# Causal mask of the self-attention scores: added by VectorE in the pass that takes each head's maximum, instead of by a mask product on TensorE, with the written-out orders laid out anew

## The chip, the core and the metric

The kernel runs on one core of one Trainium2 chip. The metric is the device time of one execution in microseconds (us); lower is better. The core has the engines TensorE (PE, with its weight loads PEld), VectorE (DVE), ScalarE (ACT), GpSimd (POOL) and SyncE (SP), which issues the transfers. They run side by side and meet at semaphores. In a steady stage the granted TensorE clock was 1.00, the 2.4 GHz level.

## What is computed

One decoder layer with layer norms behind the residual sums, for 16 batches of S = 112 rows, model width D = 256, 16 heads of 16, and a context of 375 rows per batch. Cut to what matters:

```python
# self-attention (scores already hold both of its terms and the scale)
causal = jnp.tril(jnp.ones((s, s), dtype=bool))
scores = jnp.where(causal[None, None], scores, -jnp.inf)
attn = jax.nn.softmax(scores, axis=-1)
out = jnp.einsum('bhqk,bkhd->bqhd', attn, V).reshape(b, s, H * hd)
# the layer
x = _layernorm(x + self_attention(x))
x = _layernorm(x + cross_attention(x, ctx, mask))       # keys 375, one mask for all rows
x = _layernorm(x + fp4_ffn(x))                          # blocks of 16 quantized before each product
```

## The kernel before

The work is a software pipeline over batches. In slot i the five engines work on several batches at once: self-attention of batch i+1 (`a`), the maxima of the cross-attention scores of batch i (`c`), the rest of the cross-attention of batch i-1 (`p`, `ct`), the first half of the feed-forward part of batch i-2 (`f`) and its end for batch i-3 (`ft`), while the projections of batch i+2 (`fr`) and the context keys and values of batch i+1 (`kv`) are made. Slots 3 to 13 run the same list (`slot`), the ramp (slots -2 to 2) and the drain (14 to 18) have lists of their own. Each engine has its own list, written out by hand in an order that was laid out beforehand, and works it off strictly in order; the numbers of slots and uses are known when the program is built, so every wait is on a constant.

Results of TensorE land in PSUM banks, shared in rings of two: `score` (raw scores), `prob` (scores with keys as rows), `misc` (everything else; its order of use is the table MISC_IN, MISC_ORDER, MISC_OUT). A use n of a ring may start when the reader of use n-2 has let go (`taken`), so the order of a ring ties TensorE to its readers.

Self-attention scores: heads come in four groups of four, A0 to A3. `bias_self(i, big)` writes the causal mask into the two banks of a pair of groups, as a product of an identity `identb` (bf16) and the mask `causal4` (bf16, 448 columns wide, four heads side by side), two matmuls of 448 columns. `scores_self` adds the eight head products of the pair onto it. VectorE then takes the maximum of each head's row, one reduction for a group of four heads (`max_self`). `turn_max` turns the maxima (misc use A.mT), ScalarE copies them to `mT`, GpSimd spreads them into `move_a` (`diagonal`), and a second score product with keys as rows (`turned_self`) subtracts them and masks by `shift_a`, before ScalarE takes the exponentials. The cross-attention does likewise with `max_cross`, which already adds its mask on VectorE: one custom instruction with an accumulated maximum (`tensor_tensor_reduce`) for each head of 375 columns, and a second, short one that reads the accumulator.

The feed-forward part's quantization is a chain of nine VectorE steps: `quant_x` for x (256 columns), whose end releases `turn_xq` (misc use X.xT), and `quant_h` for the two halves of h (352 columns), whose end releases `turn_hq` (hT1, hT0) of the next slot. `ctx_k` writes the context keys (K0, K1), which ScalarE copies to `kcf` and rounds, and VectorE subtracts (`ctxk_lo`).

The lines that the profile names most here: 1922 the mask product, 1933 the self scores, 1254 the self maxima, 1262 the cross maxima and their accumulator reads, 1980 the turned maxima, 2041 the context keys, 2062 the turns of xq, hq, x and att, 1162 to 1180 the quantization steps, 1344 the layer norm before it, 1310 the residual sums, 1291 the low half of xq, 633 the spreading on GpSimd.

## Time and profile before

| | |
|---|---|
| median of 3 runs | 662.46 us (661.29 to 663.1) |
| time of the profiled execution | 661.05 us |
| its span, first to last instruction | 659.2 us |
| PE busy | 592.7 us (90%) in 5682 matmuls |
| VectorE busy | 509.9 us (77%) in 1555 instructions |
| ScalarE, GpSimd busy | 294.6 us, 213.8 us |
| steady slots 3 to 13 | about 35.6 us each |

A busy PE is a modelled figure: the matmuls are pipelined, and their ends overlap with the next one's start, so the time that a piece of work costs the PE is read from start to start. What matters is what the PE waits for, slot by slot.

### The profile page before, as it was taken

Reading aid. Unit: us, or ns where it says so; the run is one execution under the profiler, and the core shown is the slowest. Engines: PE = TensorE matmul, PEld = TensorE weight load, DVE = VectorE, ACT = ScalarE, POOL = GpSimd, SP = SyncE. Lnnn points to the kernel's source line nnn. Section 1 sums busy time; section 2 is a strip of 40 time slices with the busy share of each in tenths; the row PEclk is TensorE's granted clock in tenths of the full one; section 3 lists DMA queues with packets and bytes.
Section 4 is the critical chain, followed back from the end, with each engine's and each line's share of the span. In section 5 each row is a group of like instructions: output and inputs, shape, how many; then the busy total and the mean of one; then the engine's idle time right before and its main releaser. Section 6 shows DMA issues by size and latency. Waiting matters only on the chain.

```text
span 659.2 us, 16222 instructions
## 1 busy us (share of the span) xinstructions
PE 592.7 (90%) x5682; PEld 380.1 (58%) x5682; DVE 509.9 (77%) x1555; ACT 294.6 (45%) x717; POOL 213.8 (32%) x286
## 2 busy tenths in 40 slices
PE   3687798899999999999999999999999999997964
PEld 3445465566666666666666656665666665553532
DVE  3679688896978869696968687887969696979772
ACT  1144354445454555454545455454545454442411
POOL 5244234315150524242341515051424233223001
PEclk9789899899999999999999999999999999999996
DMA  6734461515252433526251525343342512120000
GB/s 168 212 95 138 140 191 49 175 32 150 75 152 86 132 107 74 164 56 178 54 143 59 158 70 151 87 133 106 91 148 59 173 50 88 49 88 2 9 7 14
DMA packets 64464, 67.78 MB, mean 103 GB/s; under 512 B 11696, under 2 KB 55936, under 8 KB 64384
## 3 DMA queue, kind: packets, MB, share of 16 engines
q1 hardware_dynamic: 64384, 66.75, 35.1%
q8 instruction: 46, 0.75, 0.5%
q14 instruction: 34, 0.28, 0.1%
HBM read 39.72 MB, written 27.00 MB: 101 GB/s over the span
## 4 chain that ended last, share of the span: by engine, by line
PE 64%; DVE 20%; issue 8%; ACT 3%; POOL 3%; SPq 1%; DMA 1%; DVEq 0%; POOLq 0%; ACTq 0%
PE misc L2020 18%; PE prob L1960 7%; PE misc L2101 6%; PE misc L2041 5%; PE xpv L2001 5%; PE misc L2012 5%; PE score L1946 5%; DVE junk L1262 4%; PE prob L1955 4%; DVE amax L1254 2%; PE apv L1989 2%; PE misc L2054 2%; PE misc L2062 2%; DVE qt L1176 2%; DVE hq L1180 1%
## 5 line engine op out<-in xcount | busy, mean ns | idle before, releaser
L1262 DVE CUSTOM_DVE_ANT_0 junk<-score,maskbias 112x375 bf16<-112x375 f32 x256 | 128.5, 540 | 43.3 <-PE score L1946 42.8
L800 ACT ACTIVATE xP<-prob 128x448 f32<-128x448 f32 (+1 forms) x192 | 98.5, 542 | 106.8 <-PE prob L1960 106.5
L638 POOL TENSOR_TENSOR rstd<-veps,half 112x1 f32<-112x1 f32 x48 | 27.2, 576 | 295.9 <-DVE veps L1340 295.9
L2020 PE MATMUL misc<-wguT,xqT 128*112 128x352 f32 x256 | 87.2, 468 | 0.5 <-ACT xqT L764 0.5
L633 POOL TENSOR_TENSOR move_a<-mT,negeye 16x448 bf16<-16x448 f32 x64 | 60.6, 969 | 77.9 <-ACT mT L764 77.9
L633 POOL TENSOR_TENSOR move_x<-mT,negeye 16x448 bf16<-16x448 f32 x64 | 65.3, 1036 | 53.9 <-ACT mT L764 53.9
L2020 PEld LDWEIGHTS misc<-wguT,xqT 128*112 128x112 f32 x256 | 44.2, 180 | 24.6 <-issue 2.9
L1960 PE MATMUL prob<-move_x,shift_x 128*128 128x448 bf16 x192 | 54.0, 360 | 1.5 <-POOL move_x L633 1.4
L2020 PE MATMUL misc<-xwvT_s,ctxT_s 128*128 128x256 f32 (+1 forms) x192 | 52.2, 395 | 0.0
L2101 PE MATMUL misc<-wdT,hqT 128*112 128x256 f32 x192 | 49.6, 402 | 1.5 <-ACT hqT L764 1.5
L1946 PE MATMUL score<-xK,xQ 64*128 64x375 f16 x256 | 42.9, 329 | 6.7 <-DVE xmax L1262 6.2
L2001 PE MATMUL xpv<-xP,xV 128*32 128x112 f32 (+1 forms) x1536 | 47.9, 264 | 0.0
L2041 PE MATMUL misc<-ctxT_s,xwkT_s 128*128 128x375 f32 x128 | 47.7, 494 | 0.1
L2001 PEld LDWEIGHTS xpv<-xP,xV 128*32 128x32 f32 (+1 forms) x1536 | 36.5, 110 | 8.9 <-issue 8.1
L1254 DVE TENSOR_REDUCE amax<-score 112x4 f32<-112x448 f32 x64 | 37.6, 612 | 4.0 <-PE score L1933 4.0
L2101 PEld LDWEIGHTS misc<-wdT,hqT 128*112 128x112 f32 x192 | 32.8, 184 | 13.5 <-issue 6.8
L1946 PEld LDWEIGHTS score<-xK,xQ 64*128 64x128 f16 x256 | 13.1, 92 | 46.5 <-issue 32.0
L793 ACT ACTIVATE aP<-prob 112x448 f32<-112x448 f32 x64 | 31.6, 541 | 17.4 <-PE prob L1960 13.3
L1955 PE MATMUL prob<-xQ,xK 64*128 64x112 f16 x768 | 35.4, 212 | 1.9 <-ACT xP L800 1.9
L2020 PEld LDWEIGHTS misc<-xwvT_s,ctxT_s 128*128 128x128 f32 (+1 forms) x192 | 32.6, 187 | 7.7 <-issue 2.4
L1178 DVE TENSOR_TENSOR qt<-qt 112x352 f32<-112x352 f32 (+4 forms) x56 | 33.7, 602 | 0.9
L764 ACT ACTIVATE kcf<-misc 128x375 f32<-128x375 f32 x32 | 15.5, 483 | 36.2 <-PE misc L2041 36.2
(163 smaller groups left out, 1117.5 us busy)
## 6 DMA issues: line engine op xcount, KB each, us to landing
xk_dram<-xk_parts SPq DMA_DIRECT2D x64, 192.0 KB, 3.1
xK<-xk_dram SPq DMA_DIRECT2D x16, 768.0 KB, 4.6
ctxT_s<-in_ctxT SPq DMA_DIRECT2D x16, 375.0 KB, 3.8
aq_dram<-aq_parts SPq DMA_DIRECT2D x64, 64.0 KB, 2.6
ak_dram<-ak_parts SPq DMA_DIRECT2D x64, 64.0 KB, 2.1
aQ<-aq_dram SPq DMA_DIRECT2D x16, 256.0 KB, 3.6
aK<-ak_dram SPq DMA_DIRECT2D x16, 256.0 KB, 2.8
xq_dram<-xq_parts SPq DMA_DIRECT2D x64, 64.0 KB, 2.1
```

What stands on the lines that cost most here:

```text
L633: pool.tensor_tensor(dst[0:H, heads, :], mT[:, n].unsqueeze(1).to_broadcast([H, GH, S]), negeye[:, heads].unsqueeze(2).to_broadcast([H, GH ...
L800: act.activation(xP[0:KEYS[c], g % 2, c], prob[m][0:KEYS[c], 0:GH * S].rearrange("p (h q) -> p h q", h=GH), ACT.Exp).then_inc(probs.taken[ ...
L1178: done(dve.tensor_tensor(t1, t1, t2, ALU.subtract))
L1254: dve.tensor_reduce(amax[:, b.par, GH * g:GH * g + GH], score[m][0:S, 0:GH * S].rearrange("p (h k) -> p h k", h=GH), AX.X, ALU.max).then_i ...
L1262: dve.tensor_tensor_reduce(junk[:, m], score[m][0:S, 0:SC], maskbias[:], 1.0, -3.0e38, ALU.add, ALU.max, xmax[:, b.par, h:h + 1]).then_inc ...
L1946: pe.matmul(score[m[a]][:, 0:SC], xQ[rows_, b.par, at, :], xK[rows_, b.par, at, 0:SC], start=True, stop=True).then_inc(scores.full[m[a]], 1)
L1955: pe.matmul(prob[m[a]][:, n * S:(n + 1) * S], K[rows_, b.par, DT * n + big, keys], Q[rows_, b.par, DT * n + big, 0:S], start=(n == 0), sto ...
L1960: pe.matmul(prob[m[a]][:, 0:GH * S], shift_[:, keys], move[:, GH * g:GH * g + GH].rearrange("p h q -> p (h q)"), start=False, stop=True).t ...
L2001: mm = pe.matmul(xpv[VW * h:VW * h + VW, g * S:(g + 1) * S], xV[0:k, b.par, c, GH * g + h, :], xP[0:k, g % 2, c, h, :], start=(g == 0 and ...
L2020: mm = pe.matmul(misc[m][0:rows_, 0:cols], actT(c), weightT(c), start=(c == 0), stop=(c == DT - 1))
L2041: mm = pe.matmul(misc[m][:, 0:SC], xwkT_s[:, c, t * P:(t + 1) * P], ctxT_s[:, b.par, c, :], start=(c == 0), stop=(c == DT - 1))
L2101: mm = pe.matmul(misc[m][0:S, 0:D], hqT[0:k, c, :], wdT[0:k, c, :], start=(c == 0), stop=(c == IC - 1))
```

## The change

`bias_self`, `identb` and `causal4` are gone. `scores_self` now starts each bank itself, and waits itself for the banks to be free. `max_self` issues four custom instructions per group, one for each head of 112 columns, which add the 112x112 mask `causal` and take the maximum, each with its accumulator read; `junk` is widened to hold what they write. The orders of all engines, in ramp, slot and drain, and the table of the misc ring are new. SP's list moves too: in the slot, the load of x comes first, the fetch of aQ ahead of that of aK, and the store of y now stands ahead of the fetches of xK and xQ. Cut to the core:

```diff
-                pool.affine_select(out=causal4[:], in_=causal4[:], compare_op=ALU.is_ge, fill=NEG, base=0,
-                                   pattern=[[0, GH], [-1, S]], channel_multiplier=1).then_inc(consts, 1)
+                pool.affine_select(out=causal[:], in_=causal[:], compare_op=ALU.is_ge, fill=NEG, base=0,
+                                   pattern=[[-1, S]], channel_multiplier=1).then_inc(consts, 1)
...
...
 
             def max_self(i, b, g):
                 m = scores.wait_full(dve, i, f"A{g}")
-                dve.tensor_reduce(amax[:, b.par, GH * g:GH * g + GH],
-                                  score[m][0:S, 0:GH * S].rearrange("p (h k) -> p h k", h=GH),
-                                  AX.X, ALU.max).then_inc(scores.taken[m], 1)
+                for n in range(GH):
+                    h, cols = GH * g + n, slice(n * S, n * S + S)
+                    mx = dve.tensor_tensor_reduce(junk[:, m, cols], score[m][0:S, cols], causal[:], 1.0, -3.0e38, ALU.add,
+                                                  ALU.max, amax[:, b.par, h:h + 1])
+                mx.then_inc(scores.taken[m], 1)
...
-            def bias_self(i, big):
-                for a in range(2):
-                    m = scores.wait_free(pe, i, f"A{BIG * big + a}")
-                    pe.matmul(score[m][:, 0:GH * S], identb[:], causal4[:].rearrange("p h k -> p (h k)"),
-                              start=True, stop=False)
-
             def scores_self(i, b, big):
                 if big == 0:
                     pe.wait_ge(aq_in[b.par], b.round(16, 16))
                     pe.wait_ge(ak_in[b.par], b.round(16, 16))
-                m = [scores.at(i, f"A{BIG * big + a}")[0] for a in range(2)]
+                m = [scores.wait_free(pe, i, f"A{BIG * big + a}") for a in range(2)]
                 for n in range(GH):
                     for a in range(2):
                         rows_ = slice(HALF * a, HALF * a + HALF)
                         mm = pe.matmul(score[m[a]][:, n * S:(n + 1) * S], aQ[rows_, b.par, DT * n + big, :],
-                                       aK[rows_, b.par, DT * n + big, 0:S], start=False, stop=(n == GH - 1))
+                                       aK[rows_, b.par, DT * n + big, 0:S], start=True, stop=True)
                         if n == GH - 1:
...
-MISC_ORDER = ["hT1", "hT0", "q", "down", "A.mT", "X.xT", "k", "gate0", "up0", "v", "gate1", "up1", "A.out",
-              "A.att", "K0", "A.o", "V0", "X.out", "K1", "X.att", "V2", "X.o", "A.xT", "X.mT", "V1", "A.q"]
+MISC_ORDER = ["hT1", "q", "hT0", "down", "A.mT", "X.xT", "k", "gate0", "v", "up0", "gate1", "up1", "A.out", "K0",
+              "A.att", "A.o", "V0", "X.out", "K1", "X.att", "V2", "X.o", "A.xT", "X.mT", "A.q", "V1"]
...
```

In the slot's list of VectorE (`slot`), its head and its tail:

```diff
                 max_self(i, a, 0)
+                layernorm(f)
                 max_self(i, a, 1)
-                layernorm(f)
                 quant_x(f, 0)
                 quant_x(f, 1)
+                q_lo(i, fr)
                 quant_x(f, 2)
+                max_self(i, a, 2)
                 quant_x(f, 3)
-                max_self(i, a, 2)
+                max_self(i, a, 3)
                 quant_x(f, 4)
-                max_self(i, a, 3)
-                q_lo(i, fr)
...
-                quant_h(i, f, 1, 4)
+                ctxk_lo(i, kv, 0)
+                quant_h(i, f, 0, 7)
                 ctxk_lo(i, kv, 1)
                 max_cross(i, c, 7)
                 residual_cross(i, ct)
-                quant_h(i, f, 1, 5)
+                quant_h(i, f, 1, 7)
+                moments(i, ct, 1, "X.o", 0)
+                moments(i, ct, 1, "X.o", 1)
                 quant_h(i, f, 0, 8)
-                quant_h(i, f, 1, 6)
-                moments(i, ct, 1, "X.o", 0)
-                quant_h(i, f, 1, 7)
-                moments(i, ct, 1, "X.o", 1)
                 quant_h(i, f, 1, 8)
                 moments(i, ct, 1, "X.o", 2)
                 xq_lo_(i, a)
```

TensorE at the seam of two steady slots, before (from the turn of the cross maxima, `ident,xmax`, over the mask product to the second pair of self scores and what follows):

```order
L1980 MATMUL misc<-ident,xmax 16x112
L2020 MATMUL misc<-xwvT_s,ctxT_s 128x256 x2
L2012 MATMUL misc<-x1T,xwqT_s 128x112 x4
L1922 MATMUL score<-causal,identb 128x448 x2
L1933 MATMUL score<-aK,aQ 128x112 x8
L1955 MATMUL prob<-xQ,xK 128x112 x8
L1960 MATMUL prob<-move_x,shift_x 128x448 x2
L2062 MATMUL misc<-ident,hq 128x112
L2062 MATMUL misc<-ident,hq 64x112
L2062 MATMUL misc<-ident,hq 128x112 x4
L1922 MATMUL score<-causal,identb 128x448 x2
L1933 MATMUL score<-aK,aQ 128x112 x8
```

The same place in the changed kernel:

```order
L1973 MATMUL misc<-ident,xmax 16x112
L2005 MATMUL misc<-x1T,xwqT_s 128x112 x4
L2013 MATMUL misc<-xwvT_s,ctxT_s 128x256 x2
L1926 MATMUL score<-aK,aQ 128x112 x8
L1948 MATMUL prob<-xQ,xK 128x112 x8
L1953 MATMUL prob<-move_x,shift_x 128x448 x2
L2055 MATMUL misc<-ident,hq 128x112
L2055 MATMUL misc<-ident,hq 64x112
L2005 MATMUL misc<-xT_s,wqT_s 128x112 x4
L2055 MATMUL misc<-ident,hq 128x112 x4
L1994 MATMUL xpv<-xP,xV 32x112 x8
L1926 MATMUL score<-aK,aQ 128x112 x8
```

Both mask products are gone, the q projection (`xT_s,wqT_s`) and one cross value product (`xP,xV`) now stand between the first and the second pair of self scores, and the projection from x1T stands ahead of the values from ctxT.

VectorE at the same seam, before (from the cross residual `res` to the first two groups of self maxima `amax`):

```order
L1310 TENSOR_TENSOR res<-misc,x1kept 112x256
L1174 TENSOR_SCALAR qt<-qt 112x352
L1180 TENSOR_TENSOR hq<-qt,qscale 112x352
L1176 SCALAR_TENSOR_TENSOR qt<-qt 112x352
L1332 BN_STATS stats<-res 112x6
L1178 TENSOR_TENSOR qt<-qt 112x352
L1336 BN_AGGR mv<-stats 112x2
L1180 TENSOR_TENSOR hq<-qt,qscale 112x352
L1340 TENSOR_SCALAR veps<-mv 112x1
L1291 SCALAR_TENSOR_TENSOR xq_parts<-misc,xq_parts 128x2x112
L1254 TENSOR_REDUCE amax<-score 112x4 x2
```

The same place in the changed kernel (the last two rows come four times for each group):

```order
L1309 TENSOR_TENSOR res<-misc,x1kept 112x256
L1175 TENSOR_TENSOR qt<-qt 112x352
L1331 BN_STATS stats<-res 112x6
L1335 BN_AGGR mv<-stats 112x2
L1177 TENSOR_TENSOR hq<-qt,qscale 112x352 x2
L1339 TENSOR_SCALAR veps<-mv 112x1
L1290 SCALAR_TENSOR_TENSOR xq_parts<-misc,xq_parts 128x2x112
L1253 ISA junk,amax<-score,causal 112x112
L1253 ISA amax 112x1
```

The rows 1174 and 1176 of the second half of h (1171 and 1173 by the changed file's numbers) are gone from this tail; both `hq` steps now stand together, behind `mv`.

VectorE ahead of it, around the context keys, before:

```order
L1336 BN_AGGR mv<-stats 112x2
L1340 TENSOR_SCALAR veps<-mv 112x1 x2
L1301 RECIPROCAL rsum<-misc 112x16
L1262 ISA junk,xmax<-score,maskbias 112x375
L1262 ISA xmax 112x1
L1262 ISA junk,xmax<-score,maskbias 112x375
L1262 ISA xmax 112x1
L1304 TENSOR_TENSOR att<-misc,rsum 112x256
L1171 TENSOR_SCALAR qt<-qt 112x352
L1285 TENSOR_TENSOR xk_parts<-kcf,xk_parts 128x375
```

In the changed kernel:

```order
L1335 BN_AGGR mv<-stats 112x2
L1339 TENSOR_SCALAR veps<-mv 112x1
L1171 TENSOR_SCALAR qt<-qt 112x352
L1300 RECIPROCAL rsum<-misc 112x16
L1339 TENSOR_SCALAR veps<-mv 112x1
L1173 SCALAR_TENSOR_TENSOR qt<-qt 112x352 x2
L1303 TENSOR_TENSOR att<-misc,rsum 112x256
L1284 TENSOR_TENSOR xk_parts<-kcf,xk_parts 128x375
L1175 TENSOR_TENSOR qt<-qt 112x352
L1284 TENSOR_TENSOR xk_parts<-kcf,xk_parts 128x375
```

The two steps gone from the tail are here now, with two steps of the first half of h, between the two parts of the cross normalisation (`rsum`, `att`), and the seventh pair of cross maxima (`max_cross(i, c, 6)`) that stood between them has moved ahead.

## Rows read from the trace of the kernel before

**Rows 1.** The page's busy times: engine, us, share of the span, instructions.
```profile
PE 592.7 (90%) x5682; PEld 380.1 (58%) x5682; DVE 509.9 (77%) x1555; ACT 294.6 (45%) x717; POOL 213.8 (32%) x286
```

**Rows 2.** Windows: us, busy of PE, PEld, DVE, ACT, POOL; clock, DMA share, GB/s.
```profile
333.30:368.80 35.50, 34.81 (x353) 22.70 (x352) 28.36 (x92) 17.86 (x44) 11.90 (x16) 1.00 0.38 109
```

**Rows 3.** The chain that ended last: the down product, slots 3 and 12.
```profile
190.96 2.77 PE misc L2101 x12
...
511.39 2.77 PE misc L2101 x12
```

**Rows 4.** Groups by form: busy us, mean ns of one, idle before.
```profile
L1262 DVE CUSTOM_DVE_ANT_0 junk<-score,maskbias 112x375 bf16<-112x375 f32 x256 | 128.5, 540 | 43.3 <-PE score L1946 42.8 <-issue 0.2
...
L1254 DVE TENSOR_REDUCE amax<-score 112x4 f32<-112x448 f32 x64 | 37.6, 612 | 4.0 <-PE score L1933 4.0
...
L1262 DVE DVE_READ_ACCUMULATOR2_ANT xmax<- 112x1 f32 x256 | 21.1, 82 | 0.0
...
L1922 PE MATMUL score<-causal,identb 112*128 112x448 bf16 x64 | 20.2, 363 | 4.1 <-DVE amax L1254 4.1
```

**Rows 5.** PE in order of time: start us, us, what; [idle before, releaser].
```profile
336.87 0.36 PE L2062 MATMUL misc<-ident,xq 112*128 112x112 f32 x2
...
342.74 1.34 PE L2001 MATMUL xpv<-xP,xV 128*32 128x112 f32 x48
...
357.12 1.53 PE L2041 MATMUL misc<-ctxT_s,xwkT_s 128*128 128x375 f32 x4
...
361.89 0.26 PE L1980 MATMUL misc<-ident,xmax 112*16 112x112 f32 x1 [0.48 <-DVE res L1310]
...
363.74 0.54 PE L1922 MATMUL score<-causal,identb 112*128 112x448 bf16 x2
364.22 0.37 PE L1933 MATMUL score<-aK,aQ 64*128 64x112 f16 x8
...
366.06 0.36 PE L1922 MATMUL score<-causal,identb 112*128 112x448 bf16 x1
366.60 0.36 PE L1922 MATMUL score<-causal,identb 112*128 112x448 bf16 x1 [0.17 <-DVE amax L1254]
366.89 0.37 PE L1933 MATMUL score<-aK,aQ 64*128 64x112 f16 x8
```

**Rows 6.** VectorE in order of time, the same columns.
```profile
334.07 0.57 DVE L1269 SCALAR_TENSOR_TENSOR aq_parts<-misc,bq_s,aq_parts 128x112 f16<-128x112 f32 x2
...
342.55 0.55 DVE L1262 CUSTOM_DVE_ANT_0 junk<-score,maskbias 112x375 bf16<-112x375 f32 x1 [2.11 <-PE score L1946]
...
343.02 0.54 DVE L1262 CUSTOM_DVE_ANT_0 junk<-score,maskbias 112x375 bf16<-112x375 f32 x1
```

**Rows 7.** VectorE at the seam of two slots.
```profile
361.32 0.42 DVE L1310 TENSOR_TENSOR res<-misc,x1kept 112x256 f32<-112x256 f32 x1
361.66 0.24 DVE L1174 TENSOR_SCALAR qt<-qt 112x352 bf16<-112x352 bf16 x1
361.82 0.52 DVE L1180 TENSOR_TENSOR hq<-qt,qscale 112x352 f32<-112x352 f32 x1
362.25 0.52 DVE L1176 SCALAR_TENSOR_TENSOR qt<-qt 112x352 f32<-112x352 f32 x1
...
363.03 0.92 DVE L1178 TENSOR_TENSOR qt<-qt 112x352 f32<-112x352 f32 x1
...
363.98 1.14 DVE L1180 TENSOR_TENSOR hq<-qt,qscale 112x352 f32<-112x352 f32 x1
...
365.40 1.14 DVE L1254 TENSOR_REDUCE amax<-score 112x4 f32<-112x448 f32 x2
366.46 0.40 DVE L1344 TENSOR_SCALAR x<-res,mv,rstd 112x256 f32<-112x256 f32 x1
...
371.27 0.42 DVE L1180 TENSOR_TENSOR xq<-qt,qscale 112x256 f32<-112x256 f32 x1
```

**Rows 8.** GpSimd at the seam.
```profile
362.52 2.21 POOL L633 TENSOR_TENSOR move_x<-mT,negeye 16x448 bf16<-16x448 f32 x2 [2.01 <-ACT mT L764]
```

More of the change, by code:

```diff
@@ L663, in ramp @@
                 residual(at[0])
-                residual(at[1])
                 power(0, at[0])
@@ L1617, in slot @@
                 k_lo(i, fr)
+                moments(i, ft, 2, "down", 0)
+                moments(i, ft, 2, "down", 1)
                 gate_(i, f, 0)
@@ L1788, in drain @@
                 quant_x(at[14], 6)
+                moments(at[15], at[12], 2, "down", 1)
                 quant_x(at[14], 7)
@@ L1794, in drain @@
                 quant_h(at[16], at[14], 0, 1)
+                moments(at[15], at[12], 2, "down", 2)
                 quant_h(at[16], at[14], 0, 2)
@@ L1820, in drain @@
                 moments(at[16], at[15], 1, "X.o", 2)
+                moments(at[16], at[13], 2, "down", 1)
                 layernorm(at[15])
@@ L2386, in drain @@
                 pv_cross(at[15], at[14], 0, 0)
-                turned_cross(at[15], at[14], 0, 2)
+                pv_cross(at[15], at[14], 0, 1)
                 turn_hq(at[15], at[12], "hT1", range(4, IC))
                 turn_hq(at[15], at[12], "hT0", range(4))
-                pv_cross(at[15], at[14], 0, 1)
+                turned_cross(at[15], at[14], 0, 2)
+                down(at[15], at[12])
+                turn_xq(at[15], at[13])
+                gate_up(at[15], at[13], "gate", 0)
+                gate_up(at[15], at[13], "up", 0)
```

874 lines of the change are left out of this document (426 added, 448 removed), and 14 rows, old and new, of tables (MISC_IN, MISC_OUT).

## The prediction, on record before the changed kernel ran

> **What bounds the kernel now.** I read the page's busy times first, then a steady slot by windows, then the chain that ended last, then TensorE and VectorE in order of time around one seam of two slots. The page gives TensorE 90% of the span and VectorE 77% [rows 1]. That is an average, so the second view is one slot: in 35.50 us TensorE is busy for 34.81 at a granted clock of 1.00, its 2.4 GHz level, and VectorE for 28.36 [rows 2]. The chain has the same down product at 190.96 in slot 3 and at 511.39 in slot 12, nine periods of 35.60 us on average [rows 3]. Eleven such slots, 3 to 13, are 392 of the 659 us.
>
> Inside a slot TensorE waits twice in a way that the trace names: 0.48 us before the turned cross maxima, for the bank that the cross residual lets go, and 0.17 us before the second mask product of the second pair, for a self maximum [rows 5]. So the slot is TensorE's, but with little in hand over VectorE. How little, the reader sees in one loop through both engines, which I call the loop:
> - TensorE turns xq at 336.87 and comes to the end of the second context key product, K1, at 357.12 + 1.53 = 358.65: 21.78 us [rows 5].
> - From K1 ScalarE's copies and VectorE's tail lead to the next xq. It is done at 371.27 + 0.42 = 371.69: 13.04 us after K1 [rows 5, 7]. Some 0.05 us of semaphore bring it to TensorE.
> - Together 34.87 us. The period is 35.6, so the loop has 0.7 us of slack now, and TensorE does not wait for xq.
>
> **What goes from TensorE.** The first pair's mask product takes from 363.74 to the start of the self scores at 364.22, 0.48 us; the second pair's from 366.06 to 366.89, 0.83 us, its wait included [rows 5]. I leave about 0.1 us of each to the switch into the self scores, which stays: 1.1 us a slot. A TensorE that nothing else held up would have a period of 34.5 us. The scores products themselves keep number and size.
>
> **What comes to VectorE.** A reduction over a group is 612 ns long, but two stand from 365.40 to 366.46, so one costs 0.53 us [rows 4, 7]. The new form, 112 columns, has no row. The same instruction at 375 columns is 540 ns long and costs 0.47 us from start to start, its accumulator read of 82 ns included [rows 4, 6]. What a column costs I take from this instruction and a 256-column sum from PSUM, 0.34 us from 361.32 to 361.66 [rows 7]: 0.13 us for 119 columns, 1.1 ns each. 263 columns fewer leave 0.47 - 0.27 to 0.29, about 0.20 us. The bounds: if cost were proportional to columns, 0.47 x 112 / 375 = 0.14; the nearest row of this width, two operations of 112 columns that also read a bias, is 0.57 us for both with the tail of the last, 0.285 each at most, some 0.24 from start to start if that tail is as long as in the other rows [rows 6]. I take 0.20, since the opcode is the one with the 0.47. A group then costs 0.80, +0.27; four groups, +1.08 us a slot. The added instructions wait for nothing: the group's one wait stays ahead of its first.
>
> The Trainium skill, Perfetto Trace Analysis, section Optimizing Scalar/DVE Operations, speaks against this change: it gives a DVE instruction on PSUM about 125 ns of overhead and advises grouping into larger operations. By it a group of four would cost 0.97 us, and the slot would come out as in the slower rival below; this trace sides with less, 0.47 us where 375 columns by the page would be 0.52.
>
> **What the new order does to the loop.** All four groups, the layer norm and q's low half lie between the tail and xq in both orders, so the whole +1.08 is in the loop; only their order differs. The tail loses the two steps L1174 and L1176, 0.16 and 0.43 us [rows 7]. But GpSimd's first two spreads run from 362.52 to 364.73 [rows 8], and in that time the step L1178 is 0.92 us and the last hq 1.14, where the hq before them is 0.52 [rows 7]. In the new order both hq stand there and L1178 ahead of it: 0.6 more, 0.4 less. Net the tail is 0.35 shorter. The steps put ahead of K1's residue lie in time that VectorE has: it needs 28.4 + 1.1 = 29.5 of 35 us. On TensorE one value product moves out of the stretch from xq to K1, across the seam; three take 1.34 us, so about 0.40 goes [rows 5]. The loop is then 13.04 + 0.05 - 0.35 + 1.08 = 13.82 and 21.78 - 0.40 = 21.38, together 35.20 us. That is above TensorE's 34.5: TensorE will wait for xq about half a microsecond a slot, and the gain is 35.60 - 35.20 = 0.40, not 1.1. Eleven slots: -4.4 us.
>
> The first value product and the q projection between the two pairs of self scores, about 1.3 us of TensorE work, are there to cover the maxima of the first pair, 1.6 + 0.4 us with the layer norm between them. Where they fall short, TensorE waits for a second maximum, but the same delay is then missing at xq. The wait of 0.48 for the residual stays, since nothing between K1 and it has changed.
>
> **SP.** In the slot the store of y stands ahead of the fetches of xK and xQ now. It waits for the last layer norm, behind it both fetches wait. That layer norm is on ScalarE before the low half of xq is, for which the put ahead of the store waits anyhow; I add one issue and nothing to the time, since the cross scores that read both fetches come behind the k and v projections, a gate and an up product of the next slot. If that cover were gone, it would cost the issue, under half a microsecond a slot. The fetch of aQ and aK feeds the next slot, the load of x the one after.
>
> **Ramp and drain.** The page's idle TensorE time is 659.2 - 592.7 = 66.5 us [rows 1]; eleven slots of 0.7 hold 8 of it, so the rest lies in ramp and drain. There five batches have a mask product. Were TensorE the bound, they would give back 5 x 1.1 = 5.5 us; were VectorE, which also quantizes the weights there, they would cost 5 x 1.08 = 5.4. The reordering has no price in any row. I take -1, and these two as bounds.
>
> **Sum.** -4.4 - 1 = -5.4 on the profiled execution's 661.05 us (span 659.2 and 1.85 around it): 655.6. The median of the runs lies 1.4 above that execution, so 657 us.
>
> **Rivals.**
> 1. *The loop closes early, TensorE stays the bound.* For it: 0.14 us per instruction instead of 0.20 takes 16 x 0.06 = 0.96 off the loop, 34.2, below 34.5. Against it: fixed parts are seen in every short VectorE row. 11 x -1.1 = -12.1, with -1 outside: 649.5.
> 2. *Slower, by the price of the small instruction.* The loop breaks even at 0.40 / 16 = 0.025 us more than I take, 0.225 us each. At 0.24, as the operations with a bias suggest, it is 35.20 + 0.64 = 35.84, +0.24 a slot, +2.6 in eleven; with VectorE-bound ramp and drain of +1 to +5 the result is 666 to 670. Its place is the group of self maxima and then the wait for xq.
> 3. *No change.* Either the price is 0.21 to 0.225, or ramp and drain give back what the slots gain: 661 to 664.
> 4. *The freed TensorE time was covered.* If the mask product ran while TensorE had to wait anyhow, nothing is freed; the rows show it issued right behind the projection and the turned h, so only its 0.17 is such time. I count this with no change.
>
> **How the numbers follow.** A change under 0.3%, 2 us, can't be told from none here. Forecast 654 to 660.4: 0.44. Rival 1, 649 to 654: 0.17. No change, 660.5 to 664.5: 0.19. Slower: 0.20. So faster 0.61, same 0.19, slower 0.20. The range of 650 to 666 takes in the TensorE bound below and the 0.24 price above; the forecast's own is 654 to 660.
>
> **What would show it.** The custom instruction of 112 columns at about 0.20 us from start to start, 270 ns long; down products 35.2 us apart in the chain; TensorE waits before the turn of xq, released by xq; that of 0.48 unchanged; VectorE near 29.5 busy in a slot. Wrong would be: no wait at xq and a period of 34.5 (rival 1), or a long one and a period over 35.6 (rival 2), or a period as forecast with the difference in ramp or drain.

## Result: slower by 1.3%, and the profile after

The changed kernel takes 672.12 us (median of 4 runs, 670.18 to 675.07), the kernel before 662.78 us on the same chip (661.29 to 665.74). The ratio is 1.0131, 95% interval 1.0107 to 1.0155. The forecast was 657 us, within 650 to 666, with a chance of 0.20 for slower. It was wrong in direction and in range.

The profiled execution took 672.86 us, its span is 671.1 us. First the page of the changed kernel, its busy times and the group of the masked maxima:

```profile
span 671.1 us, 16558 instructions
PE 592.5 (88%) x5618; PEld 375.2 (56%) x5618; DVE 531.0 (79%) x2003; ACT 296.7 (44%) x717; POOL 219.7 (33%) x284
L1253 DVE CUSTOM_DVE_ANT_0 junk<-score,causal 112x112 bf16<-112x112 f32 x256 | 53.5, 264 | 2.4 <-PE score L1926 2.3
```

VectorE has 21 us more to do, as [rows 1] and this line show side by side. TensorE's busy time hardly moved (592.7 to 592.5), though the mask products are gone. In a steady slot at a granted clock of 1.00 it went from 34.80 us (301.38 to 336.87, before) to 34.51 (308.83 to 344.65), and over the whole execution the mean granted clock was 0.952 here and 0.970 there. Busy is a modelled figure, so it does not price what was taken out; how the rest divides between model and clock is not shown.

From the chain that ended last, the same projection from x1 (the one that starts with `misc<-x1T,xwqT_s`) in two slots nine periods apart, start and length:

```profile
190.27 0.91 PE misc L2005 x8
...
513.04 0.91 PE misc L2005 x8
```

(513.04 - 190.27) / 9 = 35.86 us, against 35.60 in [rows 3]. The first of the nine is still 36.19 long, the others are 35.82. A slip in the numbering ahead of the result: the down products at 190.96 and 511.39 in the kernel before belong to slots 4 and 13; nine periods lie between them all the same, and slots 3 to 13 are eleven.

VectorE of the changed kernel at the seam of two slots, in order of time (start, length, line and operation, waits in brackets), which answers to [rows 7]:

```profile
333.10 0.42 DVE L1309 TENSOR_TENSOR res<-misc,x1kept 112x256 f32<-112x256 f32 x1
333.44 0.52 DVE L1175 TENSOR_TENSOR qt<-qt 112x352 f32<-112x352 f32 x1
...
334.49 2.28 DVE L1177 TENSOR_TENSOR hq<-qt,qscale 112x352 f32<-112x352 f32 x2
336.70 0.14 DVE L1339 TENSOR_SCALAR veps<-mv 112x1 f32<-112x1 f32 x1
336.76 0.38 DVE L1290 SCALAR_TENSOR_TENSOR xq_parts<-misc,xq_parts 128x224 f16<-128x224 f32 x1
337.06 0.26 DVE L1253 CUSTOM_DVE_ANT_0 junk<-score,causal 112x112 bf16<-112x112 f32 x1
337.25 0.08 DVE L1253 DVE_READ_ACCUMULATOR2_ANT amax<- 112x1 f32 x1
337.25 0.26 DVE L1253 CUSTOM_DVE_ANT_0 junk<-score,causal 112x112 bf16<-112x112 f32 x1
...
343.75 0.42 DVE L1177 TENSOR_TENSOR xq<-qt,qscale 112x256 f32<-112x256 f32 x1
344.09 0.42 DVE L1309 TENSOR_TENSOR res<-misc,x 112x256 f32<-112x256 f32 x1
```

And TensorE and GpSimd in the same seam:

```profile
328.90 1.53 PE L2034 MATMUL misc<-ctxT_s,xwkT_s 128*128 128x375 f32 x4
...
334.30 2.10 POOL L630 TENSOR_TENSOR move_x<-mT,negeye 16x448 bf16<-16x448 f32 x2 [0.57 <-ACT mT L761]
337.29 0.38 PE L2055 MATMUL misc<-ident,hq 112*128 112x112 f32 x2 [0.48 <-DVE xq_parts L1290]
...
343.97 1.87 POOL L630 TENSOR_TENSOR move_a<-mT,negeye 16x448 bf16<-16x448 f32 x2 [4.66 <-ACT mT L761]
344.65 0.38 PE L2055 MATMUL misc<-ident,xq 112*128 112x112 f32 x2 [0.26 <-DVE res L1309]
```

Three things are to be read here. The masked maximum starts every 0.195 us (337.06, 337.25), so its price was forecast well. xq is done at 344.17, 13.74 us after K1's end at 330.43; forecast were 13.77. But TensorE turns xq at 344.65 only. What it waits for last is not xq but `res`, the residual of the FFN's output (FFN: the feed-forward part), which stands behind the last step of xq on VectorE. This residual reads the `misc` bank that the turn of xq needs, since a use of the ring may start when the reader of the use two before has let go, and `down` is that use. So the loop closes through the residual, 0.48 us behind xq: 14.22 + 21.60 = 35.82 us, which is the period.

### The profile page after: what moved, and what is told of

Read it like the earlier page. It is cut to its first block, busy times and chain, and to the rows that moved or that the text cites. A ratio compares the mean times of both kernels' runs of the same rounds, so it can differ in the third digit from the quotient of the medians.

```text
span 671.1 us, 16558 instructions
## 1 busy us (share of the span) xinstructions
PE 592.5 (88%) x5618; PEld 375.2 (56%) x5618; DVE 531.0 (79%) x2003; ACT 296.7 (44%) x717; POOL 219.7 (33%) x284
## 4 chain that ended last, share of the span: by engine, by line
PE 56%; DVE 29%; issue 7%; ACT 4%; POOL 1%; SPq 1%; DMA 1%; DVEq 0%; POOLq 0%; ACTq 0%
PE misc L2013 18%; PE misc L2034 6%; DVE junk L1253 6%; PE prob L1953 6%; PE score L1939 5%; PE xpv L1994 5%; PE misc L2005 5%; DVE junk L1261 4%; PE prob L1948 3%; DVE hq L1177 3%; PE misc L2055 2%; PE apv L1982 2%; DVE res L1309 2%; PE misc L2047 2%; DVE qt L1175 2%
## 5 line engine op out<-in xcount | busy, mean ns | idle before, releaser
L1261 DVE CUSTOM_DVE_ANT_0 junk<-score,maskbias 112x375 bf16<-112x375 f32 x256 | 130.0, 546 | 44.6 <-PE score L1939 44.1
L797 ACT ACTIVATE xP<-prob 128x448 f32<-128x448 f32 (+1 forms) x192 | 95.6, 541 | 76.2 <-PE prob L1953 75.9
L635 POOL TENSOR_TENSOR rstd<-veps,half 112x1 f32<-112x1 f32 x48 | 29.8, 620 | 301.0 <-DVE veps L1339 301.0
L630 POOL TENSOR_TENSOR move_a<-mT,negeye 16x448 bf16<-16x448 f32 x64 | 62.5, 1000 | 73.8 <-ACT mT L761 73.8
L630 POOL TENSOR_TENSOR move_x<-mT,negeye 16x448 bf16<-16x448 f32 x64 | 63.4, 1005 | 58.3 <-ACT mT L761 58.3
L1953 PE MATMUL prob<-move_x,shift_x 128*128 128x448 bf16 x192 | 56.1, 366 | 0.4 <-POOL move_x L630 0.4
L2013 PE MATMUL misc<-xwvT_s,ctxT_s 128*128 128x256 f32 (+1 forms) x192 | 53.7, 403 | 2.5 <-DVE res L1309 2.2
L1253 DVE CUSTOM_DVE_ANT_0 junk<-score,causal 112x112 bf16<-112x112 f32 x256 | 53.5, 264 | 2.4 <-PE score L1926 2.3
L2034 PE MATMUL misc<-ctxT_s,xwkT_s 128*128 128x375 f32 x128 | 49.9, 514 | 0.4
L1277 DVE SCALAR_TENSOR_TENSOR ak_parts<-misc,bk_s,ak_parts 128x112 f16<-128x112 f32 x32 | 9.2, 328 | 30.7 <-ACT ak_parts L761 30.7
```

The source lines that it names most:

```text
L630: pool.tensor_tensor(dst[0:H, heads, :], mT[:, n].unsqueeze(1).to_broadcast([H, GH, S]), negeye[:, heads].unsqueeze(2).to_broadcast([H, GH ...
L797: act.activation(xP[0:KEYS[c], g % 2, c], prob[m][0:KEYS[c], 0:GH * S].rearrange("p (h q) -> p h q", h=GH), ACT.Exp).then_inc(probs.taken[ ...
L1253: mx = dve.tensor_tensor_reduce(junk[:, m, cols], score[m][0:S, cols], causal[:], 1.0, -3.0e38, ALU.add, ALU.max, amax[:, b.par, h:h + 1])
L1261: dve.tensor_tensor_reduce(junk[:, m, 0:SC], score[m][0:S, 0:SC], maskbias[:], 1.0, -3.0e38, ALU.add, ALU.max, xmax[:, b.par, h:h + 1]).th ...
L1953: pe.matmul(prob[m[a]][:, 0:GH * S], shift_[:, keys], move[:, GH * g:GH * g + GH].rearrange("p h q -> p (h q)"), start=False, stop=True).t ...
L2013: mm = pe.matmul(misc[m][0:rows_, 0:cols], actT(c), weightT(c), start=(c == 0), stop=(c == DT - 1))
```

## Experiments

Every kernel below keeps the reference's whole computation. "Mask" says which engine adds the causal mask, "order" whose written-out lists are used. I write "order of before" and "new order" for the written-out lists and the ring's table; K1 and "turn" (of xq, on TensorE) as in the prediction. The times are medians, and each ratio is to the kernel before on the same chip. The last four columns are medians over slots 4 to 12 of one profiled execution, worked out from the rows in order of time, as above; they are good to about 0.03 us.

| kernel | mask, order | time, us | ratio (95%) | K1 to xq done | xq done to turn | turn to K1 | period |
|---|---|---|---|---|---|---|---|
| before | TensorE, before | 662.8 to 664.2 | | 13.04 | 0.72 | 21.78 | 35.55 |
| changed | VectorE, new | 672.12 | 1.0131 (1.0107 to 1.0155) | 13.74 | 0.48 | 21.60 | 35.82 |
| old_order_dve_mask | VectorE, before | 685.3 | 1.0325 (1.0287 to 1.0363) | 15.00 | 0.48 | 21.76 | 37.24 |
| old_order_both | both, before | 676.17 | 1.0192 (1.0149 to 1.0235) | 14.27 | 0.48 | 21.76 | 36.52 |
| new_order_pe_mask | TensorE, new | 669.21 | 1.0075 (1.0049 to 1.0101) | 13.19 | 0.91 | 21.57 | 35.67 |
| old_ends_new_slot | VectorE, new slot only | 666.38 | 1.0044 (1.0025 to 1.0062) | 13.74 | 0.48 | 21.60 | 35.82 |
| old_dve_xq_first | VectorE, before, edited | 683.7 | 1.0304 (1.0261 to 1.0348) | 13.78 | 1.52 | 21.73 | 37.06 |
| new_resid | VectorE, new, edited | 668.97 | 1.0089 (1.0057 to 1.0121) | 13.94 | 0.06 | 21.62 | 35.62 |
| early_hq | VectorE, new, edited | 662.72 | 0.9986 (0.9967 to 1.0006) | 13.07 | 0.48 | 21.59 | 35.15 |
| before_early_hq | TensorE, before, edited | 660.84 | 0.9956 (0.9933 to 0.9979) | 12.99 | 0.48 | 21.81 | 35.31 |
| new_ramp | VectorE, new but for the drain | 668.56 | 1.0084 (1.0062 to 1.0106) | 13.73 | 0.49 | 21.60 | 35.82 |
| new_drain | VectorE, new but for the ramp | 668.37 | 1.0073 (1.0051 to 1.0095) | 13.74 | 0.48 | 21.60 | 35.83 |
| best2 | VectorE, old ends, slot edited | 657.43 | 0.9916 (0.9894 to 0.9937) | 13.28 | 0.06 | 21.63 | 34.97 |
| best2_pe | TensorE, as best2 | 660.30 | 0.9954 (0.9935 to 0.9973) | 13.69 | 0.06 | 21.62 | 35.37 |

### The exchange alone, the order alone

**old_order_dve_mask**: the changed kernel's functions, all lists and the ring's table of before, without the mask product's calls.

```diff
-MISC_ORDER = ["hT1", "q", "hT0", "down", "A.mT", "X.xT", "k", "gate0", "v", "up0", "gate1", "up1", "A.out", "K0",
-              "A.att", "A.o", "V0", "X.out", "K1", "X.att", "V2", "X.o", "A.xT", "X.mT", "A.q", "V1"]
+MISC_ORDER = ["hT1", "hT0", "q", "down", "A.mT", "X.xT", "k", "gate0", "up0", "v", "gate1", "up1", "A.out",
+              "A.att", "K0", "A.o", "V0", "X.out", "K1", "X.att", "V2", "X.o", "A.xT", "X.mT", "V1", "A.q"]
...
```

> The mask moved to VectorE as in the change, but every engine keeps the order of before. Theory 1, the loop that closes over the misc bank: in before TensorE turns xq 13.40 + 0.14 us after K1 at the earliest, since its bank is let go by the feed-forward residual behind xq, and 21.78 us later K1 is done, 35.3 against a period of 35.6. The four groups add 16 x 0.20 - 4 x 0.53 = 1.08 us, so the period becomes 36.4 and eleven slots cost +9, with 0 to +4 in ramp and drain: 670 to 676 us. Rival, TensorE is the bound and the new order alone is to blame: the 1.1 us of mask product per slot come back, 650 to 660 us.

**old_order_both**: the kernel before, with its mask product, and the masked maxima as well (the mask is added twice, which leaves the result as it is).

```diff
-                dve.tensor_reduce(amax[:, b.par, GH * g:GH * g + GH],
-                                  score[m][0:S, 0:GH * S].rearrange("p (h k) -> p h k", h=GH),
-                                  AX.X, ALU.max).then_inc(scores.taken[m], 1)
+                for n in range(GH):
+                    h, cols = GH * g + n, slice(n * S, n * S + S)
+                    mx = dve.tensor_tensor_reduce(junk[:, m, cols], score[m][0:S, cols], causal4[:, 0], 1.0, -3.0e38, ALU.add,
+                                                  ALU.max, amax[:, b.par, h:h + 1])
+                mx.then_inc(scores.taken[m], 1)
```

> The order of before with its mask product on TensorE kept, and the maxima taken as in the change (the mask is added twice, the result is the same). Only the price of the small VectorE instructions is added. Theory 1: the mask product lies outside the stretch from xq to K1, so the period is the same 36.4 as without it, and the time is within 3 us of the kernel of old order with the mask on VectorE alone, 672 to 678 us. Rival, TensorE bound: it is 12 us or more slower than that kernel.

Both are slower than the changed kernel, and the one that still has TensorE's mask product is 9 us the faster of the two. My expectation missed the first by 9 us (670 to 676); it had the second's time (672 to 678), but not its distance from the first (within 3 us). No count of "less work on TensorE, more on VectorE" gives that. The rows do. In old_order_dve_mask, the last step of xq and GpSimd's first spread of the self maxima:

```profile
309.27 0.92 POOL L630 TENSOR_TENSOR move_a<-mT,negeye 16x448 bf16<-16x448 f32 x1 [4.84 <-ACT mT L761]
309.32 1.15 DVE L1177 TENSOR_TENSOR xq<-qt,qscale 112x256 f32<-112x256 f32 x1
310.40 0.41 DVE L1309 TENSOR_TENSOR res<-misc,x 112x256 f32<-112x256 f32 x1
```

The same in old_order_both:

```profile
307.89 0.42 DVE L1180 TENSOR_TENSOR xq<-qt,qscale 112x256 f32<-112x256 f32 x1
308.04 2.85 POOL L633 TENSOR_TENSOR move_a<-mT,negeye 16x448 bf16<-16x448 f32 x3 [5.04 <-ACT mT L764]
308.24 0.42 DVE L1312 TENSOR_TENSOR res<-misc,x 112x256 f32<-112x256 f32 x1
```

Issued 0.05 us behind the spread's start, the step takes 1.15 us; issued 0.15 us ahead of it, 0.42 us. That is 0.73 us in each such slot, all of the difference of the periods (37.24 - 36.52 = 0.72) and, over eleven slots, 8 of the 9 us. Without its mask product TensorE is earlier at the turned maxima, so the spread is, and it meets the step. The 0.97 us that the masked maxima alone cost (36.52 - 35.55) are nearly the 1.08 us that the forecast put into the loop: the loop had little slack before.

One slot of old_order_dve_mask gives the counter-test inside a single execution. There the step happened to be issued 0.04 us ahead of the spread:

```profile
346.61 0.43 DVE L1177 TENSOR_TENSOR xq<-qt,qscale 112x256 f32<-112x256 f32 x1
346.65 2.06 POOL L630 TENSOR_TENSOR move_a<-mT,negeye 16x448 bf16<-16x448 f32 x2 [4.93 <-ACT mT L761]
```

It took 0.43 us, and TensorE turned xq 36.55 us after the turn before, where the slots on either side have 37.24. The lists are the same in all of them, so neither the order nor the missing mask product explains the 0.7 us; only the step's place against the spread differs.

The Trainium skill, SBUF — State Buffer, section Who interferes with whom, has the rule: a VectorE instruction with two inputs in SBUF contends with a GpSimd instruction that reads SBUF, whichever issues first keeps the shared port for its whole length and the other is blocked, and one with at most one SBUF input does not contend unless it runs in a mode that uses both of VectorE's ports, which `tensor_scalar` can enter. The rows agree in kind: 0.87 us were left of a spread of 0.92 us when the step came, and it ended 0.73 us late, somewhat less than a full block would make it, while the masked maxima, whose scores lie in PSUM, keep their 0.195 us in the changed kernel's spreads from 337.45 on. The layer norm's product, a `tensor_scalar` from SBUF to SBUF, is slowed too (0.69 to 1.11 us in all kernels but before, instead of 0.40); in which mode it ran no trace shows.

**new_order_pe_mask**: the new order with the functions of before, the mask product right ahead of the score products.

```diff
+                bias_self(i, 0)
                 scores_self(i, a, 0)
```

> The orders of the change, but with the mask product on TensorE (right ahead of each pair of self scores) and one reduction per group, as before. Theory 1: the loop is 35.8 - 1.1 = 34.7 us, so TensorE sets a period of 35.3 to 35.7 again and the slots cost nothing; what ramp and drain lost in the change by their order stays, what they lost by VectorE's work goes: 662 to 670 us. Rival, the order of the slots is at fault: a period of 35.8 or more stays, 670 us or more.

669.21 us: in the new order the exchange is worth +0.15 us a slot (35.82 against 35.67), and at the same time the order alone is 5 us slower than that of before (669.21 against 664.18). **old_ends_new_slot**, the changed kernel with ramp and drain in the order of before, tells where:

> The changed kernel with the ramp and the drain of the old order (the mask product left out of them) and the slot of the new order. Theory 1: the slots keep a period of 35.82, +2.4 us in eleven; the rest of the change's +12, 6.3 in the ramp and 3.6 in the drain, is by the order of these lists and goes but for the VectorE work of five batches, at most 5 us: 664 to 670 us. Rival, the ends lose by VectorE's work and not by order: 670 to 674 us, as the changed kernel.

666.38 us: 5.7 us of the 9.3 lie in the order of ramp and drain.

### Ramp and drain

**new_ramp** and **new_drain** each give one end back. Their edits are the lists and MISC_OUT, or MISC_IN, of before.

> The changed kernel's slot and first stretch (its ramp), with the drain in the order of before. Together with old_ends_new_slot (both ends of before, 666.38 us) and the changed kernel (both ends new, 672.1 us) it splits the 5.7 us that the ends' order costs. From the profiled executions: drain behind slot 13's down product 151.6 us in the changed kernel, 148.8 us in old_ends_new_slot (2.8 us), down product of slot 3 at 160.90 and 158.47 us (2.4 us). Theory 1: the two ends lose about half each, so 668 to 670.5. Rival (the first stretch's difference lies in the clock that one execution was granted, and the drain holds all of it): within 1 us of 666.4.

> The opposite: first stretch of before, slot and drain of the changed kernel. Theory 1: 668 to 670.5 as well, the two losses adding up to 5.7 us. Rival (the drain holds all of it): 671 to 673.

Against old_ends_new_slot the new ramp costs 0.40% (1.0084 against 1.0044) and the new drain 0.29%, some 2.7 and 1.9 us, each give or take 1.9; both together, in the changed kernel, 0.87%, 5.8 us give or take 2. So they fit the first theory, about half in each end; the exact split these runs can't tell.

What the loss consists of the traces show in part. The windows view (length, busy time of PE, PEld, DVE, ACT, POOL, granted clock, DMA share, GB/s), changed kernel:

```profile
40.00:80.00 40.00, 31.16 (x226) 20.20 (x225) 30.62 (x104) 15.48 (x37) 8.97 (x13) 0.84 0.50 138
80.00:120.00 40.00, 36.04 (x401) 23.06 (x402) 35.03 (x150) 20.14 (x49) 16.95 (x20) 0.90 0.39 110
...
580.00:620.00 40.00, 32.46 (x258) 17.97 (x256) 32.38 (x94) 14.18 (x33) 9.92 (x14) 0.87 0.20 57
```

The kernel before:

```profile
40.00:80.00 40.00, 31.88 (x222) 20.10 (x222) 30.07 (x80) 15.42 (x37) 10.84 (x14) 0.96 0.49 143
80.00:120.00 40.00, 36.38 (x449) 23.58 (x447) 34.52 (x92) 22.37 (x54) 20.64 (x22) 1.00 0.41 115
...
580.00:620.00 40.00, 34.52 (x359) 19.61 (x356) 30.08 (x92) 16.31 (x40) 10.03 (x12) 0.96 0.13 38
```

And new_drain, whose drain has the same lists as the changed kernel's:

```profile
580.00:620.00 40.00, 30.56 (x294) 16.77 (x298) 34.08 (x95) 14.84 (x34) 11.64 (x12) 1.00 0.20 57
```

From slot 13's down product to the end the changed kernel takes 151.6 us (519.51 to 671.1) and new_drain, by the same lists, 149.1 (517.51 to 666.6); the difference goes with the clock, 0.87 against 1.00. The lists of before take 148.8 in old_ends_new_slot. The ramp is alike: slot 3's down product starts at 160.90 in the changed kernel and at 158.19 in new_ramp, by the same lists. In the kernel before it starts at 154.63 and in before_early_hq, whose ramp is the same list for list, at 158.49, and there too the clocks differ. These are before_early_hq's windows, to be laid beside the kernel before's 0.96 and 1.00:

```profile
40.00:80.00 40.00, 32.75 (x208) 19.90 (x206) 28.03 (x75) 14.62 (x35) 10.28 (x13) 0.84 0.49 144
80.00:120.00 40.00, 36.60 (x384) 24.04 (x383) 31.97 (x91) 19.54 (x48) 17.77 (x17) 0.92 0.36 104
```

So the execution that stands ahead of the prediction had a fortunate ramp, and the lower clock of the changed kernel's ramp is no proof against its order. All executions together say more about the ends: the mean granted clock is 0.945 to 0.959 in the changed kernel's four and 0.963 to 0.970 in the ten of old_ends_new_slot. In new_order_pe_mask, with the new ends, three runs at 0.969 to 0.975 took 665.3 to 666.2 us, the other seven, at 0.953 to 0.962, 668.6 to 671.5. New_drain is at 0.964 to 0.974 and still takes 666.5 to 669.5. How much of the 5.7 us is waiting, how much the lower clock, and which brings the other about, these runs don't separate.

### The slot

**old_dve_xq_first** tests the collision: old_order_dve_mask, with xq's last steps ahead of the next q's low half.

```diff
                 max_self(i, a, 3)
-                q_lo(i, fr)
                 quant_x(f, 5)
                 quant_x(f, 6)
                 quant_x(f, 7)
                 quant_x(f, 8)
+                q_lo(i, fr)
```

> This is old_order_dve_mask (the order of before, mask added by VectorE), with the two parts of the next q (0.57 us) moved in VectorE's slot from ahead of the last four steps of the FFN input's quantizing to behind them. In old_order_dve_mask the last of these steps took 1.15 us, where it takes 0.42 us in the kernels before and old_order_both; it is issued 0.05 us after GpSimd has begun a spread (309.32 and 309.27), while in old_order_both it starts 0.15 us ahead of the spread. Theory 1 (a two-input VectorE instruction on on-chip float32 that is issued during a spread runs at under half its speed, and one issued ahead of it does not): the step starts 0.5 us earlier, falls back to 0.42 us, the slot shortens by about 0.7 to 1.2 us, and 685.3 us becomes 672 to 678. Rival (the missing mask product on TensorE is itself what costs old_order_dve_mask its 9 us over old_order_both): the time stays at 683 to 687.

The time stayed at 683.7 us, as the rival had it, yet not for its reason:

```profile
350.06 0.42 DVE L1177 TENSOR_TENSOR xq<-qt,qscale 112x256 f32<-112x256 f32 x1
350.41 0.57 DVE L1268 SCALAR_TENSOR_TENSOR aq_parts<-misc,bq_s,aq_parts 128x112 f16<-128x112 f32 x2
351.12 0.26 PE L1973 MATMUL misc<-ident,amax 112*16 112x112 f32 x1 [1.19 <-DVE aq_parts L1268]
351.75 3.60 POOL L630 TENSOR_TENSOR move_a<-mT,negeye 16x448 bf16<-16x448 f32 x4 [6.09 <-ACT mT L761]
352.00 0.36 PE L2055 MATMUL misc<-ident,xq 112*128 112x112 f32 x2
```

The step is back at 0.42 us and xq is done 1.22 us sooner behind K1 (13.78 against 15.00): 0.73 for the step, and about 0.5 since the parts of q now stand behind it. TensorE has no use for it: ahead of the turn of xq it turns the maxima, whose bank the low half of q has to release, and that is late now by 1.19 us. The step's own part of the theory holds, its effect on the time does not: the gain went into a new wait.

**new_resid**: the changed kernel, with the wait that the forecast missed taken away.

```diff
-                quant_x(f, 8)
                 residual_ffn(i, ft)
+                quant_x(f, 8)
```

> The changed kernel with one pair swapped in VectorE's slot: the residual of the FFN's output stands ahead of the last quantizing step of the next FFN input, not behind it. TensorE's turn of that input waited 0.26 us for this residual behind the step (344.09 with 0.42 us, turn at 344.65). Theory 1 (the collision with GpSimd's spread decides): the last step is then issued at about 344.1, after the spread's start at 343.97, and takes 1.15 instead of 0.42 us; the slot grows by about 0.6 us and the time goes to 676 to 681. Rival (the residual's wait is what the slot lost, and taking it away gives it back): the period falls from 35.8 to 35.6 or less, 668 to 671.

My theory lost. The step started 0.01 us ahead of the spread, not 0.13 behind it, and was not slowed:

```profile
340.91 0.42 DVE L1309 TENSOR_TENSOR res<-misc,x 112x256 f32<-112x256 f32 x1
341.24 0.41 DVE L1177 TENSOR_TENSOR xq<-qt,qscale 112x256 f32<-112x256 f32 x1
341.25 3.87 POOL L630 TENSOR_TENSOR move_a<-mT,negeye 16x448 bf16<-16x448 f32 x4 [4.66 <-ACT mT L761]
341.71 0.20 PEld L2055 LDWEIGHTS misc<-ident,xq 112*128 112x128 f32 x2 [0.48 <-DVE xq L1177]
```

TensorE waits for xq itself now and turns it 0.06 us after. The period fell by 0.20 us, to 35.62, so the wait for the residual behind xq was real and in the loop.

**early_hq**: the changed kernel, with both last steps of h ahead of the spreads.

```diff
                 quant_h(i, f, 0, 7)
+                quant_h(i, f, 0, 8)
                 ctxk_lo(i, kv, 1)
                 max_cross(i, c, 7)
                 residual_cross(i, ct)
                 quant_h(i, f, 1, 7)
+                quant_h(i, f, 1, 8)
                 moments(i, ct, 1, "X.o", 0)
                 moments(i, ct, 1, "X.o", 1)
-                quant_h(i, f, 0, 8)
-                quant_h(i, f, 1, 8)
```

> The changed kernel with the last quantizing step of both halves of h moved ahead in VectorE's slot: the first half's into the idle 0.27 us ahead of the second part of xk, the second half's straight behind the step ahead of it, so that both are issued ahead of GpSimd's spreads at 334.30. Now the two take 2.21 us from issue to the next one, unslowed 0.43 us each. Theory 1 (VectorE's tail of the slot lies on the loop, so what the spreads cost there counts): 1.1 to 1.4 us less on VectorE in each slot; the period falls from 35.8 until another limit ends it, at 34.6 to 35.3; time 660 to 667. Rival (the loop is TensorE's, and the tail only fills its waits): 670 to 673.

9.4 us less from moving two lines, period 35.15. The slots make 7.4 us of it (11 times 0.67); in this execution the drain was also shorter, 148.4 us from slot 13's down product (512.73) to the end against 151.6, by the same lists and at a granted clock of 1.00 against 0.87 from 580 to 620 us. Of the 1.35 us saved on the two steps (2.21 to twice 0.43), 0.67 reached the period; part of the rest was paid back at once, since the layer norm's product, also from SBUF to SBUF, now falls into the second pair of spreads and takes 1.02 us instead of 0.69:

```profile
331.36 0.53 DVE L1177 TENSOR_TENSOR hq<-qt,qscale 112x352 f32<-112x352 f32 x1
331.60 1.97 POOL L630 TENSOR_TENSOR move_x<-mT,negeye 16x448 bf16<-16x448 f32 x2
...
334.06 1.86 POOL L630 TENSOR_TENSOR move_x<-mT,negeye 16x448 bf16<-16x448 f32 x2
334.12 1.02 DVE L1343 TENSOR_SCALAR x<-res,mv,rstd 112x256 f32<-112x256 f32 x1
```

**before_early_hq**: the same idea in the kernel before.

```diff
                 quant_h(i, f, 1, 4)
+                quant_h(i, f, 1, 5)
+                quant_h(i, f, 0, 8)
+                quant_h(i, f, 1, 6)
                 ctxk_lo(i, kv, 1)
                 max_cross(i, c, 7)
                 residual_cross(i, ct)
-                quant_h(i, f, 1, 5)
-                quant_h(i, f, 0, 8)
-                quant_h(i, f, 1, 6)
-                moments(i, ct, 1, "X.o", 0)
                 quant_h(i, f, 1, 7)
-                moments(i, ct, 1, "X.o", 1)
                 quant_h(i, f, 1, 8)
+                moments(i, ct, 1, "X.o", 0)
+                moments(i, ct, 1, "X.o", 1)
```

> The kernel before, its mask product and maxima kept, with the same idea in its own slot: steps 5 and 6 of the second half and step 8 of the first stand ahead of the second part of xk, where VectorE waited 0.81 us, and steps 7 and 8 of the second half stand right behind the cross residual; in the kernel before the steps in the spreads took 0.92 and 1.14 us for 0.46 and 0.43 unslowed. Theory 1: the tail shortens by 1.2 to 1.8 us, the period falls from 35.6 to between 34.5 and 35.0, the time to 650 to 657. Rival (TensorE has no use for it): 660 to 664.

Faster, by 0.44%, but a quarter of what I expected: the period is 35.31. VectorE now waits 0.86 us for xq's low half, and its layer norm product takes 1.10 us in the spreads, so again a good part moved into the next wait.

### The exchange in an order that suits it

**best2** is the changed kernel with ramp and drain of before and the edits of early_hq and new_resid; **best2_pe** is the same order with the mask product and the plain maxima.

> The mask added by VectorE, with all that the runs so far gave: both ends in the order of before (666.38 us for the changed kernel), the last quantizing steps of h ahead of GpSimd's spreads (9.4 us off the changed kernel in early_hq, its period 35.15), and the FFN's residual ahead of the last step of the next input (3.2 us off, period 35.6 from 35.8). Theory 1, the three add up: 672.1 - 5.7 - 9.4 - 3.2 = 653.8; less likely all of it, since the second and third act on the same loop: 653 to 658, period 34.9 to 35.15. Rival (TensorE is the limit at 35.1 and the residual gives nothing more): 657 to 660.

> The same order, instruction by instruction, with the mask product on TensorE (ahead of each score product) and the plain maxima on VectorE instead of the masked ones. It tells what the exchange is worth where neither has an order of its own. Theory 1 (the loop runs through VectorE, which does 1.1 us less in a slot here, and TensorE 1.1 us more, so the loop gets shorter on one and longer on the other): within 3 us of best2, 651 to 659. Rival (TensorE is the bound in this order, and the exchange then pays what it set out to): 8 us or more above best2. Other rival (VectorE is): 5 us or more below.

best2 is the fastest kernel of all, 657.43 us, 0.84% below before, at the upper end of what I expected; the plain sum of the three parts, 653.8, took in the 3 us by which early_hq's drain was shorter. best2_pe is 2.9 us slower. The two intervals just touch, but on the same chip its fastest run (659.05) is above best2's slowest (658.45), and the steady slots show it, with a period of 35.37 against 34.97. So the exchange is worth -0.40 us a slot here, by coincidence the number of the forecast; eleven of them are 4.4 us, against 2.9 between the medians. VectorE's 1.08 us of saved work did not shorten best2_pe's slot. It waits instead, for TensorE, which comes later by its mask products: 1.53 us in the three rows below, where best2 has one wait of 0.17 us in the same stretch.

```profile
332.12 0.62 DVE L1254 TENSOR_REDUCE amax<-score 112x4 f32<-112x448 f32 x1 [0.71 <-PE score L1933]
335.58 0.62 DVE L1254 TENSOR_REDUCE amax<-score 112x4 f32<-112x448 f32 x1 [0.24 <-PE score L1933]
339.03 0.42 DVE L1310 TENSOR_TENSOR res<-misc,x 112x256 f32<-112x256 f32 x1 [0.58 <-PE misc L2101]
```

## Why the prediction was wrong, point by point

**The price of the new instruction was right.** 0.195 us from start to start for a forecast of 0.20, 264 ns long for 270. So rival 2 gave the right sign, and with 35.84 us even the right period, by a mechanism that did not occur: its 0.24 us is refuted, and the match is luck.

**From K1 to xq the sum was right, by luck**: xq is done 13.74 us after K1 for 13.77. Both last steps of h ran in the spreads, as the step on the new order's tail said, but cost more there. From the cross residual's start to the first maximum are 3.96 us (333.10 to 337.06), before 4.08 (361.32 to 365.40): the tail is shorter by 0.12, not 0.35. From the first maximum to the end of xq are 7.11 us (to 344.17), before 6.29 (to 371.69): +0.82, not +1.08, though the layer norm's product in it rose from 0.40 to 0.69. What made this stretch cheaper than the new instructions' price no run separates.

**The loop was closed at the wrong place.** The step "the loop has 0.7 us of slack now" took the turn of xq 0.05 us behind xq. The turn also needs the bank of `down`, and its reader, the residual, comes after xq on VectorE. In the kernel before TensorE is 0.72 us behind xq without a named wait, but 0.48 of it are necessary: 13.04 + 0.48 + 21.78 = 35.30 us, and the slack was 0.25 us. This is the step that failed: the slack was put at 0.7 us and measured 0.25. With that one term the forecast's own sum is 35.63 instead of 35.20, no gain at all. old_order_both says the same from the other side: the masked maxima alone lengthen the slot by 0.97 us. And new_resid, where the residual no longer stands behind xq, gets 0.20 us of it back.

**TensorE's stretch shrank by 0.18 us, not 0.40** (21.78 to 21.60). A value product did leave it, but in each slot of the new order TensorE waits for VectorE's `gat` ahead of the first up product: v now stands between gate0 and up0 in the ring, so up0's bank is that of gate0. In the order of before it is that of k, and no such wait is in its slots. The changed kernel:

```profile
348.58 0.86 PEld L2013 LDWEIGHTS misc<-wguT,xqT 128*112 128x112 f32 x4 [0.23 <-DVE gat L1377]
```

The two terms, 0.43 at xq and 0.22 here, less the 0.03 from K1 to xq, are the 0.62 us by which 35.82 missed 35.20. Over eleven slots +2.4 us came in place of -4.4.

**Ramp and drain, "I take -1", were +7 us.** Of these 5.7 come from their order (old_ends_new_slot). The rest is what the exchange itself costs there: old_ends_new_slot is 0.44% or 2.9 us above before, less 2.4 in the slots leaves 0.5 us, give or take 1.2, so nothing that could be told from none. The bounds of -5.5 and +5.4 were both about the exchange, and "the reordering has no price in any row" left the larger part unpriced. That is why the range, too, was missed.

**"All of it in the loop, only the order differs" missed that order decides.** The same exchange cost +1.69 us a slot in the order of before (37.24 against 35.55), +0.15 in the new one and -0.40 in that of best2. A sum of durations could not see this; the collisions with the spreads and the rings' releases could only be read by laying both lists against the times of GpSimd.

**Rival 1** (TensorE the bound at 34.5) never came: with everything found here the loop is still at 34.97, and the weight load of xq's turn waits 0.48 us for xq. **Rival 4** said that the freed time had been covered by waits before. That is not so, but TensorE spends it in new ones: the waits that the trace names in a steady slot rose from 0.65 us (0.48 + 0.17) to 1.45 (0.48 for the cross residual, unchanged as forecast, 0.48 ahead of the turned hq, 0.26 for the residual behind xq, 0.23 for `gat`). The one ahead of hq no step of the prediction had: in the new ring hT1 takes the bank of A.q, whose reader on VectorE is xq's low half `xq_parts`; in the order of before it takes that of V1. It lies outside the stretch from xq to K1.

**The step on SP held** as far as the traces go: from slot 4 to slot 12 no engine is named as waiting for a transfer, before or after.

## What to carry to other kernels

When an engine "has slack" towards another, work the slack out to the last release that the waiting instruction needs, banks of a ring included, not to the data it reads: the wait that is already met leaves no mark in the trace. When work is moved between two engines that are tied in one loop, its price is set by the order of both, so test the exchange with the order held fixed, and the order with the exchange undone. An instruction on a busy engine's loop that can collide with a helper engine belongs ahead of the helper's start or behind its end: two moved lines were worth more here (9.4 us, 7.4 of them in the slots) than the whole exchange (2.9 us).

## What the runs showed of the hardware that I had not expected

A small GpSimd operation on 16 partitions, 0.92 us long, delays a VectorE product of 112 partitions: 0.42 us became 1.15, a pair of 0.43 us steps took 2.21 us, and the layer norm's product went from 0.40 us, its length outside the spreads too, to as much as 1.11. A start 0.01 us ahead of the spread was enough to escape it, in all eleven slots of new_resid and of best2. The norm's product also kept its 0.40 us where it started 0.25 us ahead of the end of a spread (366.46, the kernel before), but not where it started 0.05 us ahead of one's end with the next right behind (334.00, before_early_hq, 1.10 us). Maxima that read PSUM, masked or plain, and the norm's statistics kept their length inside the spreads.

The same lists in ramp or drain ran 2.5 to 3.9 us apart in two executions, with mean granted clocks of 0.87 and 1.00 over the same 40 us of a drain and of 0.84 and 0.96 over those of a ramp (1.00 is the 2.4 GHz level), so that one profile does not price an end of the kernel to better than that.
